# Layer-2 attention by head groups: second scores five units behind the first, the softmax sum carried as a logarithm in the row vector, split projections and new banks

## The reference

```python
def _L2_attn_ref(x, WQ_w, WQ_b, WK_w, WK_b, WV_w, WV_b, WO_w, WO_b):
    NH, HD = 16, 32
    q = (x @ WQ_w.T + WQ_b).reshape(b, s, NH, HD).transpose(0, 2, 1, 3)
    ...                                   # k, v the same
    scores = jnp.einsum('bhqd,bhkd->bhqk', q, k) * (1.0 / math.sqrt(HD))
    scores = jnp.where(causal, -jnp.inf, scores)
    attn = jax.nn.softmax(scores, axis=-1)
    out = jnp.einsum('bhqk,bhkd->bhqd', attn, v)
    return out.transpose(0, 2, 1, 3).reshape(b, s, h) @ WO_w.T + WO_b

def _L2_xattn_ref(q, latent_kv, Wq, Wkv_expand, Wout):   # latent_kv: (4, 512, 128)
    k, v = jnp.split(latent_kv @ Wkv_expand.T, 2, axis=-1)
    ...                                   # the same causal softmax attention, 16 heads of 32, no biases
```

## Time and profile before

| | |
|---|---|
| median of three runs | 5124.7 us |
| profiled execution | 5129.0 us, its span 5127.8 us |
| TensorE busy in the span | 4467.1 us (87%) |
| VectorE, ScalarE, GpSimd busy | 2998.9, 1684.2, 1697.6 us |
| mean granted clock of TensorE | 0.93 of full speed |

### The profile page before, as it was taken

The page is one execution under the profiler, slowest core; times in us unless marked ns, Lnnn a source line. Parts: engine busy times, 40 slices in busy tenths (PEclk is TensorE's granted clock), DMA queues, the critical chain, the costliest instruction groups (busy, mean ns, idle before and its releaser), DMA issues.

```text
span 5127.8 us, 65483 instructions
## 1 busy us (share of the span) xinstructions
PE 4467.1 (87%) x22744; PEld 2365.1 (46%) x22744; DVE 2998.9 (58%) x5723; ACT 1684.2 (33%) x3306; POOL 1697.6 (33%) x1861
## 2 busy tenths in 40 slices
PE   7996888899999758887999888849999999798688
PEld 6773222244445543554333333325555555343466
DVE  5885777678876986884555565642332333456622
ACT  1112676622113324664222222212112111355432
POOL 1224222000115863552011112455555554211511
PEclk9997999999998678999999999879999999899899
DMA  4330000010000002000012010118999996400000
GB/s 139 98 93 15 2 2 2 35 55 1 0 0 1 1 10 113 2 1 29 25 29 61 25 45 27 26 29 209 245 233 238 217 224 129 143 1 17 3 15 19
DMA packets 154390, 327.66 MB, mean 64 GB/s; under 512 B 25841, under 2 KB 39665, under 8 KB 152498
## 3 DMA queue, kind: packets, MB, share of 16 engines
q1 hardware_dynamic: 106370, 222.50, 13.4%
q0 software_dynamic: 46976, 100.56, 10.1%
q10 hardware_dynamic: 720, 0.40, 0.0%
HBM read 377.91 MB, written 79.30 MB: 89 GB/s over the span
## 4 chain that ended last, share of the span: by engine, by line
PE 64%; DVE 17%; ACT 6%; POOL 5%; issue 4%; DMA 3%; SPq 0%; DVEq 0%; ACTq 0%; POOLq 0%
PE ps L205 59%; PE ps L210 4%; DVE arena L867 2%; ACT arena L2406 2%; ACT arena L841 1%; DVE ps L1386 1%; DVE ps L1409 1%; DMA moe_y<-arena 1%; DVE arena L2432 1%; POOL moe_slots L2133 1%; DVE arena L248 1%; ACT arena L834 1%; ACT arena L1771 1%; DVE arena L1378 1%; DVE arena L2448 1%
## 5 line engine op out<-in xcount | busy, mean ns | idle before, releaser
L205 PE MATMUL ps<-arena 128*128 128x512 f32 (+14 forms) x18488 | 3918.9, 455 | 369.3 <-ACT arena L1786 50.6
L205 PEld LDWEIGHTS ps<-arena 128*128 128x128 f32 (+3 forms) x18488 | 1842.2, 165 | 2250.2 <-issue 1199.9
L210 PE MATMUL ps<-arena 128*128 128x128 f32 (+2 forms) x3232 | 421.1, 270 | 253.3 <-DVE arena L266 54.7
L210 PEld LDWEIGHTS ps<-arena 128*128 128x128 f32 (+2 forms) x3232 | 344.0, 140 | 425.0 <-issue 200.4
L2891 POOL DMA_INDIRECT moe_y<-arena x191 | 304.9, 1596 | 303.6 <-DVE arena L2860 236.4
L256 POOL TENSOR_SCALAR arena<-arena 128x1 f32<-128x1 f32 x160 | 52.7, 330 | 925.1 <-DVE arena L250 922.4
L2406 ACT ACTIVATE arena<-ps 128x1024 f32<-128x1024 f32 (+3 forms) x256 | 166.2, 701 | 576.2 <-PE ps L205 576.2
L867 DVE TENSOR_REDUCE arena<-ps 128x2 f32<-128x1024 f32 x256 | 303.8, 1218 | 85.9 <-PE ps L205 85.1
L2432 DVE TENSOR_REDUCE arena<-ps 128x2 f32<-128x256 f32 (+3 forms) x256 | 198.8, 819 | 260.4 <-PE ps L205 260.4
L2843 DVE SCALAR_TENSOR_TENSOR arena<-ps,arena 128x128 f32<-128x128 f32 x382 | 103.5, 312 | 411.8 <-ACT arena L2830 409.9
L841 ACT ACTIVATE arena<-ps 128x512 f32<-128x512 f32 x512 | 277.6, 597 | 129.2 <-PE ps L205 126.6
(11 more groups left out here) (312 smaller groups left out, 3939.8 us busy)
## 6 DMA issues: line engine op xcount, KB each, us to landing
arena<-in_L_ffn_gu SPq DMA_DIRECT2D x191, 768.0 KB
arena<-in_L_ffn_dn SPq DMA_DIRECT2D x191, 256.0 KB
arena<-in_L_ffn_dn SPq DMA_DIRECT2D x191, 128.0 KB
arena<-in_L_ffn_w SPq DMA_DIRECT2D x64, 256.0 KB
moe_y<-arena SPq DMA_DIRECT2D x34, 256.0 KB
arena<-in_L_ffn_w_gate SPq DMA_DIRECT2D x32, 256.0 KB
arena<-in_L_ffn_w_up SPq DMA_DIRECT2D x32, 256.0 KB
arena<-in_L_ffn_w_down SPq DMA_DIRECT2D x32, 256.0 KB
```

The lines of the kernel that those rows point to most:

```text
L205: return self.nc.tensor.matmul(out, lhsT, rhs, start=start, stop=stop, skip_group_check=True)
L210: return self.nc.tensor.transpose(out, in_, ident[0:n, 0:n])
```

## The change

1. **Order of the first scores.** A unit's number now counts head groups outside for both kinds of scores. When four units are done, the row vector of one head group is complete, and second scores follow with LAG = 5. QT and KT become single buffers; `NM` now holds one head group, copied four times with a block mask (`BLK`), so that a plain `ONE` can stand for `SEL`.
2. **Mask and sums.** The causal mask is no more added by products on TensorE: VectorE's `tensor_tensor_reduce` adds it while it writes the negated scores of one head to `SR` and takes their minimum (four passes a unit for two reductions). ScalarE then exponentiates these rows and sums them (step `sums`, four a unit), and after four units takes the logarithm. `maxparts` subtracts it from the negative maximum, so that the second scores come out as finished log probabilities: the products with `ONE` in `pv`, the reciprocal and the bank `ZB` go; `over` becomes a copy.
3. **Scaling.** The factor 32^-0.5 moves from the exponential into Q's evacuation and bias.
4. **Banks.** `Q`, two banks (4 and 5), serves q, self attention's k and v, and the output tiles. `R` is now one bank (6) for transpositions, cross attention's k and v, and routing; `OB` moves to bank 7.
5. **Plan of projections.** A table (`plan`) sets each projection in a slot ahead of (`place` 0) or behind (`place` 1) the second scores; nearly every slot has two products of a projection between first and second scores. A projection's evacuation is a step of its own (`... kept`) in the next slot. V products stand behind the second scores, no more ahead of them. Most output tiles of a batch come in slots 23 to 35 after the batch's first slot (before: 38 to 47).
6. **Ternary work** runs in slots 10 to 85, with two empty steps of the transfers after each 16 tiles; one table load for exponential and logarithm is named at the start of the stage.

Where instructions stand now. Each row is a run of equal instructions of the program: line, operation, operands with the output's shape, and how many. First TensorE in the middle of self attention, before, units with 256 and then 384 keys. L205 is every product, L210 every transposition; an output of 128 x keys with four products is a unit's first scores, 128x128 x4 the mask, 32 x N x8 V products and sums (or 32 x N x4 V products alone), 128 x N x8 second scores, 128x512 x2 half a projection, 128x128 alone the transposition of the row vector.

The diff, cut to its core:

```diff
@@ l2_attn
-    S, R, OB, ZB = k.banks(0, 2, 2), k.banks(4, 2), k.banks(6, 1), k.banks(7, 1)
-    LAG = 17
+    S, Q, R, OB = k.banks(0, 2, 2), k.banks(4, 2), k.banks(6, 1), k.banks(7, 1)
+    LAG = 5
...
+    def whole(t, what, n, apart=False):
+        put(t, 0, what + " begins", n)
+        put(t + apart, 1 - apart, what, n)
+        soon(t + apart + 1, what + " kept", n)
+        return t + apart
+    soon(80, "routes", 0)
+    for b in range(8):
+        for m in range(4):
+            if b or m:
+                t = 16 * b + 4 * m - 8 if b else m - 1
+                whole(t, "q", 4 * b + m, b >= 4)
...
+        for t4 in range(4):
+            n = 4 * b + t4
+            t = 16 * b + ((23, 26, 27, 38)[t4] if b < 7 else 23 + t4)
+            if t4 == 3 and 2 <= b < 7:
+                t -= 4
+            elif t4 == 2 and 2 <= b < 7:
+                t += 3
+            t = whole(t, "out", n, 2 <= b < 7 and t4 > 0)
+            soon(t + 2, "x", n)
+            if n >= NT:
+                for lag, what in ((3, "route"), (4, "logits"), (5, "exp"), (6, "rank"), (4, "store")):
+                    soon(t + lag, what, n - NT)
...
@@ order(): a slot
             if t < 128:
                 yield "first", t
+            if u % 4 == 0 and 0 < t <= 128:
+                yield "maxrows", t // 4 - 1
+            for what, n in sorted(late.get(t, ()), key=lambda w: not w[0].endswith("kept")):
+                yield what, n
...
+            if 10 <= t < 86:
+                yield "ternary", t
+            if t < 128:
+                yield "sums", t
                 if u % 4 == 3:
                     yield "maxparts", t // 4
+            before, after = plan.get(t, ((), ()))
+            yield from before
+            if 0 <= t - LAG < 128:
+                yield "second", t - LAG
             n = t - LAG - 2
             if 0 <= n < 128:
                 yield "pv", n
                 if n % 4 == 3:
                     yield "over", n // 4
+            yield from after
@@ tensor()
             elif what == "first":
-                t4, m = divmod(u, 4)
+                m, t4 = divmod(u, 4)
...
-                s = [S.take("s1", n, j, by=((dve, "mx", n, j),)) for j in range(2)]
+                s = [S.take("s1", n, j, by=((dve, "tt", 4 * n + 2 * j + 1),)) for j in range(2)]
...
-                for g in range(4):
-                    t = k.mm(s[g // 2][:, g % 2, keys - P:keys], k.idb, k.mq, False, True)
...
             elif what == "second":
-                pe.wait_ge(dve, "mr", 4 * b + 3)
+                pe.wait_ge(dve, "mr", n // 4)
...
-                    t = k.mm(s[g // 2][:, g % 2, 0:512 - q0], SEL[heads[g], m, :], NM[b % 2][heads[g], q0:512], False, True)
+                    t = k.mm(s[g // 2][:, g % 2, 0:512 - q0], ONE[heads[g], :], NM[n // 4 % 2][heads[g], q0:512], False, True)
...
-                for g in range(4):
-                    t = k.mm(zb[heads[g], q0:512], ONE, PT[n % 4][:, g, 0:512 - q0], kt == 0, kt == 3)
@@ scalar()
+        nc.scalar.preload_act_table_set("natural_log_exp_and_others")
...
+            elif what == "sums":
+                i, t4 = divmod(n, 4)
+                keys, _ = seen(t4)
...
+                for g in range(4):
+                    s = SR[(4 * n + g) % 8][:, 0:keys]
+                    act.wait_ge(dve, "tt", 4 * n + g)
+                    nc.scalar.activation(s, s, ACT.Exp, bias=MX[:, i % 2, g, t4:t4 + 1], scale=-1.0,
+                                         accum_out=ZS[:, i % 2, g, t4:t4 + 1]).then_inc(*act.done("e", 4 * n + g))
+                if t4 == 3:
...
+                    nc.scalar.activation(LZ[:, i % 2], ZS[:, i % 2], ACT.Ln).then_inc(*act.done("lz", i))
@@ vector()
             elif what == "first":
...
-                for j in range(2):
-                    nc.vector.tensor_reduce(MX[:, i % 2, 2 * j:2 * j + 2, m], S.of("s1", n, j)[:, :, 0:keys], AX.X, ALU.max, negate=True
+                for g in range(4):
+                    h = 4 * n + g
+                    dve.wait_ge(pe, "s1", n, g // 2)
+                    dve.wait_ge(act, "e", h - 8)
+                    nc.vector.tensor_tensor_reduce(SR[h % 8][:, 0:keys], S.of("s1", n, g // 2)[:, g % 2, 0:keys], MASK[:, 512 - keys:512],
+                                                   -1.0, 3.0e38, ALU.add, ALU.min, MX[:, i % 2, g, t4:t4 + 1]).then_inc(*dve.done("tt", h))
             elif what == "maxparts":
-                dve.wait_ge(dve, "mx", 4 * n + 3, 1)
+                dve.wait_ge(act, "lz", n)
...
+                nc.vector.tensor_tensor(nb, MX[:, n % 2], LZ[:, n % 2], ALU.subtract).then_inc(*dve.done("nb", n))
...
             elif what == "over":
-                nc.vector.reciprocal(RZ, ZB.of("z", n)).then_inc(*dve.done("rz", n))
...
-                nc.vector.tensor_tensor(OT[b % 2][:, m, :], OB.of("o", n), RZ, ALU.mult).then_inc(*dve.done("ot", n))
+                nc.vector.tensor_copy(OT[b % 2][:, m, :], OB.of("o", n)).then_inc(*dve.done("ot", n))
```

More of the change, by code:

```diff
@@ L2166, in seen @@
         return i % 4 * P + P, i % 4 * P
[L2168 to L2177 removed]
+    plan, late = {}, {}
@@ L2184, in order @@
             yield what, 0
-        for t in range(128 + LAG + 16):
+            yield what + " kept", 0
+        for t in range(max(late) + 1):
             b, u = divmod(t, 16)
@@ L2270, in tensor @@
             if what == "ternary":
-                next(part, None) if n >= LOADED else None
+                next(part, None) if n >= 12 else None
             elif what == "xt":
@@ L2295, in tensor @@
                 else:
+                    pe.wait_ge(dma, "w_k", 1)
                     pe.wait_ge(dma, "ct", b - 4)
+                    r = R.take(what, n, by=((act, what, n),))
                     t = k.mm(r, WK[:, 0, m * P:m * P + P], CT[b - 4], True, True)
@@ L2411, in vector @@
     def vector():
-        dve.wait_ge(dma, "sel")
-        nc.vector.tensor_copy(SEL, stg).then_inc(*dve.done("sel"))
+        dve.wait_ge(dma, "blocks")
         dve.wait_ge(pool, "ns0")
+        nc.vector.tensor_copy(MASK[:, 3 * P:4 * P], k.mq).then_inc(*dve.done("mask"))
+        dve.wait_ge(pool, "mask0")
+        dve.wait_ge(dve, "mask")
         part = ternary_dve(k, R)
@@ L2418, in vector @@
             if what == "ternary":
-                next(part, None) if n >= LOADED else None
-            elif what == "v" and n < NT:
+                next(part, None) if n >= 12 else None
+            elif what == "v kept" and n < NT:
                 b, t4 = divmod(n, 4)
@@ L2424, in vector @@
                 dve.wait_ge(pe, "pv", 16 * (b - 2) + 15)
[L2425 removed]
+                nc.vector.tensor_tensor(V[b % 2][:, t4, :], Q.of("v", n), BV, ALU.add).then_inc(*dve.done("v", n))
             elif what == "first":
[L2427 to L2433 removed]
+                i, t4 = divmod(n, 4)
@@ L2458, in vector @@
                     dve.wait_ge(pool, "xb", n)
-                nc.vector.tensor_tensor(k.zb[n % 4], x, R.of("y", n), ALU.add).then_inc(*dve.done("z", n))
+                nc.vector.tensor_tensor(k.zb[n % 4], x, Q.of("y", n), ALU.add).then_inc(*dve.done("z", n))
                 k.norm_stats(n)
```

180 lines of the change are left out of this document (79 added, 101 removed).

## The result

The changed kernel takes 4988.7 us (median of four runs, 4987.68 to 4991.54), beside 5123.0 for the kernel before (four runs): ratio 0.9735, 95% interval 0.9723 to 0.9747, so 134 us faster. Forecast: 4955, range 4905 to 5035. The sign is right and the time lies in the range; the gain is 34 us smaller than forecast. The profiled execution took 4987.7 us, its span is 4986.4, 141.4 less than before.

The account below looks back on a forecast made before the run. TensorE was taken as the bound, busy 853.2 of 959.5 us. Savings of 33 (self attention), 63 (cross attention), 64 (from unit 128) and 11 (scatters) sum to 171, giving 4958 in the profile, forecast 4955; range 4905 to 5035.

Parts of the forecast that it names:

- What TensorE is relieved of: TensorE's products with ones (77 us) and mask products (47 us) go, together 124 us of 853 busy.
- The rule on tiling modes: Mask products: one change of tiling mode per unit, which drains the array, also goes; whole 0.41 us saved, 5 us more.
- Order and plan: Whole stage: the part of the 171 us saving beyond the 124 us of removed TensorE products, 47 us.
- moved-in work: Units 0 to 63: second scores and V products of 12 units, 22 us; output tiles 10, less 3 of projections.
- Units 0 to 63: Self attention: from 430.5 to 397 us, with busy 380, idle 14 and 3 for a shared bank pair; saving 33.
- Units 64 to 127: Cross attention: from 441 to 378 us, with busy 320 plus 3 and idle 55; saving 63.
- B: Cross attention: ScalarE and VectorE in series hold the old pace; the 63 us saving is lost, 5020 us; chance 0.14.
- B's sign: Cross attention: TensorE would wait for line 2431's exponentials most of all.
- D: Group end: TensorE stands still 6.3 us before the row vector's transposition, 32 times, 202 us; slower, 5160 us; chance 0.05.
- C: Cross attention: TensorE's clock at 0.87 adds 32 us, 4987 us; 5040 with more waits; chance 0.03 beyond the main range.
- E: ScalarE: exponential and logarithm alternate 32 times with two table loads each, 82 us, 5035 us; chance 0.01.
- F: Up to unit 127: no waits at all, 55 + 14 us less, 4889 us; chance 0.05.

Follow-up runs that it names:

- experiment 2: Removed TensorE work put back into the changed kernel: mask products 5011.2 us, each V product issued twice 5028.4, both 5052.1.
- Experiment 3: Changed kernel with the half projection between first and second scores put behind the second scores and V products: 5195.1 us, ratio 1.0135.
- experiment 4: Changed kernel, first-batch slots without projection filled with unread products: 4988.2 us; its projections spread instead: 4985.7; V products put in empty places as well: 5001.3.

## Why the prediction came out as it did

- **What TensorE is relieved of, 124 us: the step that failed.** The rows were read rightly, their worth was not. The ones measure 0.58 us per unit by rows (173.2 to 99.5 us over the stage; 0.60 taken). In the stage they are 45.3 to 57.8 us of busy time and 24.9 to 34.6 of its length, for 77: the rest covered waits. The masks, taken at 0.37 us a unit, are 0.17 to 0.24 of busy time there (22.1 and 30.5 over 128 units) and 17.4 to 27.7 us of its length (22.5 and 25 by the medians, under the low bound of 27). Together 54 us of the stage, or 63 of the span, for 124.
- **The rule on tiling modes.** The forecast let the mask row's excess over its streaming time speak for the Trainium skill's drain ("TensorEngine Tiling (Array Packing)", Key Properties: a change of tiling mode drains the array). By that rule 0.41 us a unit should have gone. The kernel before without masks has one change of mode less per unit and is 0.24 us a unit less busy, little over the 0.21 of streaming; the rest of the row was overlap of records. With the masks put back (0.17) half a projection or a transposition over 128 rows and 128 columns follows them in nearly every slot, as it would without them, so that run adds almost no change of mode. Neither run shows a drain. The difference of the two, 8.4 us or 0.07 a unit, is what they leave open for one; it was not isolated.
- **Order and plan: 78 us by the spans, the forecast held 47** (171 less 124). Twelve fewer units in flight and output tiles earlier were right, and worth more than was said: slot 128 to the last scatter was forecast at 100 us and took 101.6, but the forecast had counted 11 us of removed ones there, and experiment 2 finds none; the order alone brings the 76. Ahead of slot 128, 29 us of moved-in work was to be paid in full; with all removed work put back, slot 128 nevertheless comes at 3271, where before it came at 3278.5. Experiment 3 shows that this pace hangs on the half projection between the scores. But before, the V and ones products and in part of the slots a half projection stood at that place too, so it does not show what the new order gains over the old.
- **Luck.** The two errors of 61 and 31 us have opposite signs, and 30 are left. That the time lies 34 us from the forecast and well inside the range is due in part to this.
- **By stretches.** Units 0 to 63: 424 for 397. TensorE is busy 388.3 (380 in the sum) and idle 36.0 (17). Of the 27 us 17 are in the first batch (116.8, where an even quarter is 99), though its first five slots have no second scores yet. Its slots without a half projection were overlooked, while the last batch's were priced at 10 us; but experiment 4 filled them and got no more than 3 us by the medians, so their lack is not shown to be the loss. Units 64 to 127: 386 for 378, with TensorE busy 336.7 (323) and idle 49.2 (55): there the waits were forecast well, and the busy time fell by less than the rows promised.
- **Rivals.** B (one behind the other on ScalarE and VectorE) is half there: of the stage's engines TensorE's weight loads wait most for L2431, as B's sign was named, and cross attention returns only a quarter of what is removed. The forecast set an average unit loop of 4.7 us against TensorE's 5.4; a unit takes 6.0, with TensorE busy 5.3 of it, and no run measured the loop itself. But B's price was not paid, and shortening the sums brings at most 10 us. D did not come: TensorE's products wait 3.2 us in all for L688, its weight loads for the transposition 4.6. Its place was wrong too: what reaches the sign is not the group end but the middle of every slot (experiment 3). C came only in the last batch (0.88). E: one table load. The Trainium skill ("ScalarE: Activation LUTs", Table sets) puts exponential and logarithm in one set; the trace agrees, with the single load of 1283 ns. F is out.
- **Signs that held:** ScalarE 522.8 us busy to slot 128 (530), VectorE 468 (479 before), a cross batch 96.5 us on average (94), bf16 products 32. **Signs that did not:** from unit 0 to the last V product 839 us (800), and the groups 128\*32 hold 99.5 us (75), 0.78 a unit where the halved rows gave 0.66.

What stays open: which hand-over limits cross attention now. Every single change tried there moved it by under 10 us or made it slower, near the 6 us by which executions differ. And the same products are 34.5 us less busy in the new order (4467.1 before, 4432.6 with both put back), 24 of it in the stage. TensorE is busy at half clock for 72.7 us of the stage before and 51.4 with both put back, which makes up some 11 us (an estimate: half of the difference); the rest was not isolated.

## To carry to other kernels

Price removed work by the busy time of the whole engine without it and by what it covers, not by its group's row: here 124 us of priced rows were 82 of busy time in the stage and 54 of its length (87 and 63 over the whole program). Where two engines hand banks to and fro, look at what stands between the two takes of a bank pair; the same instructions with that filling moved behind cost 206 us, more than the whole change brings. Filling must be balanced between both waits: with the halves behind, the weight loads' wait for L2431 fell from 99.5 to 14.7 us while the one for L2474 rose from 80.5 to 243.1. And compare stretches that contain the change, not only whole times: what lies ahead of unit 0 moved by up to 9 us from one kernel to another.

## What the runs showed of the hardware

- The busy times of neighbouring groups overlap: of 512 mask products' 52.5 us only 31.4 are theirs alone, and without them the engine was busy 31.8 us less.
- The granted clock rose from 0.73 and 0.81 to 0.95 and 1.00 by ten added 512-column products, with no change of the time that can be told: the added work found room in the waits and in what the faster clock gave back. Where waits were made longer (experiment 3) it fell from 1.00 to 0.91 in whole self batches, and the same products took 54.1 us more in the stage.
- The sum that an exponential accumulates takes a read of its own of 187 ns (x256, 47.9 us in cross attention); the next exponential starts beside it, 0.71 us after the start of the one before at 512 columns.
